# Rows of C copied by four DMAs each, and the first group's softplus summed in PSUM

## What is computed

```
delta = softplus(dt @ dt_proj.T + dt_proj_b)
A = -exp(A_log)
for each position t:
    dA = exp(delta_t[:, None] * A)
    h  = dA * h + (delta_t * u_t)[:, None] * B_t[None, :]
    y_t = sum over the states n of h[:, n] * C_t[n]
y = (y + u * D) * silu(z)
```

## Time and profile before

| | us |
|---|---|
| median of three runs | 427.69 |
| lowest and highest | 424.73, 428.63 |
| the profiled execution | 426.04 |
| its span in the profile | 424.3 |

### The profile page before, as it was taken

The page is one execution under the profiler, slowest core; times in us unless marked ns, Lnnn a source line. Parts: engine busy times, 40 slices in busy tenths (PEclk is TensorE's granted clock), DMA queues, the critical chain, the costliest instruction groups (busy, mean ns, idle before and its releaser), DMA issues.

```text
span 424.3 us, 11081 instructions
## 1 busy us (share of the span) xinstructions
PE 368.8 (87%) x4065; PEld 254.5 (60%) x4065; DVE 306.4 (72%) x631; ACT 286.9 (68%) x600; POOL 166.5 (39%) x142
## 2 busy tenths in 40 slices
PE   5799999999999597989499775998978989999996
PEld 4577777777755243444154342453954579888885
DVE  2869887698664989888269889985758957555554
ACT  3588899999967868759646793359974364444443
POOL 8314132232201438833985899970722400000000
PEclk9969999999999999999979999999999989999998
DMA  7120000002314272462222222200020001111111
GB/s 160 9 21 8 2 3 1 0 0 56 76 28 108 106 175 101 129 160 98 102 103 102 103 80 102 105 12 0 14 65 2 2 1 23 19 20 22 21 22 27
DMA packets 28496, 23.23 MB, mean 55 GB/s; under 512 B 20928, under 2 KB 22720, under 8 KB 28464
## 3 DMA queue, kind: packets, MB, share of 16 engines
q1 hardware_dynamic: 28068, 22.77, 19.8%
q10 hardware_dynamic: 396, 0.05, 0.1%
HBM read 2.00 MB, written 1.61 MB: 9 GB/s over the span
## 4 chain that ended last, share of the span: by engine, by line
PE 38%; DVE 24%; issue 16%; ACT 9%; POOL 8%; DMA 3%; SPq 1%; DVEq 1%; ACTq 1%; POOLq 0%
PE pair L1683 6%; DVE pair L1976 3%; PE pair L1174 3%; POOL hC L542 3%; PE pair L1185 3%; PE pair L1134 3%; DVE stats L1757 3%; PE pair L1299 2%; DVE Ts L1867 2%; PE pair L1193 2%; PE pair L1671 2%; DMA vec<-in_L_conv_b_qkv 2%; PE pair L1156 2%; PE pair L1352 2%; PE pair L1228 2%
## 5 line engine op out<-in xcount | busy, mean ns | idle before, releaser
L542 POOL TENSOR_TENSOR hC<-Hs,Cs 128x784 f32<-128x784 f32 x31 | 59.6, 1929 | 38.4 <-DVE Hs L1988 17.3
L510 POOL TENSOR_TENSOR Km<-Ks,mask 128x784 f32<-128x784 f32 x16 | 24.1, 1508 | 71.0 <-ACT Ks L717 71.0
L1352 PE MATMUL pair<-hC,ident 128*128 128x392 f32 x128 | 48.6, 504 | 1.3 <-POOL hC L542 1.2
L1861 DVE TENSOR_REDUCE mx<-pair 128x8 f32<-128x392 f32 x64 | 33.0, 556 | 19.3 <-PE pair L1134 19.2
L1976 DVE TENSOR_TENSOR pair<-DU,pair 128x392 f32<-128x392 f32 x64 | 35.6, 556 | 15.3 <-PE pair L1348 15.1
L1683 PE MATMUL pair<-hst,BD 128*128 128x112 f32 x224 | 37.7, 299 | 2.1 <-DVE Rt L2241 0.4
L1174 PE MATMUL pair<-ident,Pr 113*113 113x113 f32 x256 | 37.3, 280 | 2.5 <-issue 1.6
L1174 PEld LDWEIGHTS pair<-ident,Pr 113*113 113x113 f32 x256 | 31.2, 184 | 12.8 <-issue 12.0
L1348 PE MATMUL pair<-BCf,sel 96*128 96x392 bf16 x64 | 21.8, 343 | 16.6 <-DVE Hs L1988 9.7
L1988 DVE TENSOR_TENSOR_SCAN Hs<-dA,Hs,pair 128x392 f32<-128x392 f32 x32 | 33.0, 1030 | 3.6
L1683 PEld LDWEIGHTS pair<-hst,BD 128*128 128x128 f32 x224 | 30.0, 195 | 9.1 <-DVE hst L2235 5.2
(11 more groups left out here) (254 smaller groups left out, 840.8 us busy)
## 6 DMA issues: line engine op xcount, KB each, us to landing
Cs<-BCf SPq DMA_DIRECT2D x32, 392.0 KB
SX<-XP SPq DMA_DIRECT2D x16, 336.8 KB, 5.9
XT<-in_x SPq DMA_DIRECT2D x4, 392.0 KB, 7.0
out<-Os SPq DMA_DIRECT2D x28, 56.0 KB, 1.7
AD<-Aa SPq DMA_DIRECT2D x4, 196.0 KB
NB<-in_L_conv_x_proj_w SPq DMA_DIRECT2D x4, 3.0 KB
DW<-in_L_conv_dw SPq DMA_DIRECT2D x4, 1.1 KB
W<-in_L_conv_w_qkv ACTq DMA_DIRECT2D x1, 48.0 KB
```

What stands on the lines that cost most here:

```text
L542: eng.tensor_tensor(hC[:, i % NHC, :], Hs[:, i % NHS, :], Cs[i % NCS][:, :], ALU.mult).then_inc(v_c, 1)
L1352: return eng.matmul(STATES[:, h, :], ident[:, :], src[:, columns(h)], start=first, stop=last)
L1861: eng.tensor_reduce(mx[:, g, :], banks[g][:, 0:392].rearrange("p (m k) -> p m k", k=WT), AX.X, ALU.max).then_inc(max_r, 1)
```

## The change

Each row of C is copied by four DMAs, one for each image, instead of one. All waits for the copies count four times the increments. In the first group's softplus, max(x, 0) stays in PSUM where x lay. The remainder is made behind the attention's last residual instead of ahead of it; it is subtracted before the wait for the logarithm, and the logarithm is added last, which writes `DL`. The first `total` waits for that (`v_dl`), since it overwrites the PSUM pair.

```diff
@@ -437,7 +437,9 @@
                         eng.wait_ge(c_["xB"], c + 1)
                     if i >= NCS:
                         eng.wait_ge(v_c, i - NCS + 1)
-                    eng.dma_start(Cs[i % NCS][:, :], bcast(BCf[3 * C + n:P:DS, c % 2, :], 1, C)).then_inc(s_cs[i % NCS], 16)
+                    for g in range(G):
+                        row = 3 * C + DS * g + n
+                        eng.dma_start(Cs[i % NCS][C * g:C * g + C, :], bcast(BCf[row:row + 1, c % 2, :], 1, C)).then_inc(s_cs[i % NCS], 16)
 
             shifted_copies(0)
             shifted_copies(1)
@@ -535,7 +537,7 @@
 
                 for n in states:
                     i = DS * c + n
-                    eng.wait_ge(s_cs[i % NCS], 16 * (i // NCS + 1))
+                    eng.wait_ge(s_cs[i % NCS], 16 * G * (i // NCS + 1))
                     eng.wait_ge(v_s, 2 * i + 2)
                     if i >= NHC:
                         eng.wait_ge(y_s, i - NHC + 1)
@@ -617,7 +619,7 @@
                     scaled(2)
                     pads()
                     times_c(3, 5, 6)
-                    eng.wait_ge(s_cs[(DS * J - 1) % NCS], 16 * (DS * J // NCS))
+                    eng.wait_ge(s_cs[(DS * J - 1) % NCS], 16 * G * (DS * J // NCS))
                     eng.wait_ge(v_b, 2 * DS * J)
                     eng.wait_ge(v_c, DS * J - 1)
                     eng.memset(AD[:], 0.0).then_inc(t_zz, 1)
@@ -1359,7 +1361,7 @@
                     if n == 0 and c:
                         eng.wait_ge(v_y2, c)
                     elif n == 0:
-                        eng.wait_ge(a_m, 1)
+                        eng.wait_ge(v_dl, 1)
                     for h in range(2):
                         ins = add_up(hC[:, i % NHC, :], h, n == 0, n == DS - 1)
                     ins.then_inc(y_s, 1)
@@ -1955,17 +1957,18 @@
             def first_rows():
                 eng.wait_ge(p_["xB"], 1)
                 eng.tensor_copy(halves(BCf[:, 0, :]), result("xB", 0)).then_inc(c_["xB"], 1)
-                remainder(0)
 
             eng.wait_ge(c_["delta"], 2)
-            eng.tensor_scalar(halves(DL[:, 0, :]), result("delta", 0), vec[:, V_DTB:V_DTB + 1], 0.0, ALU.add, ALU.max).then_inc(a_m, 1)
+            first = result("delta", 0)
+            eng.tensor_scalar(first, first, vec[:, V_DTB:V_DTB + 1], 0.0, ALU.add, ALU.max).then_inc(a_m, 1)
             dve_att(17, 1, first_rows)
+            remainder(0)
             eng.wait_ge(a_m, 1)
+            eng.wait_ge(v_cc, 1)
+            eng.tensor_tensor(first, first, halves(rest), ALU.subtract).then_inc(g_ml, 1)
             eng.wait_ge(a_l, 1)
-            eng.tensor_tensor(DL[:, 0, :], DL[:, 0, :], sp[:, SP_L, :], ALU.add).then_inc(g_ml, 1)
             eng.wait_ge(g_ml, 1)
-            eng.wait_ge(v_cc, 1)
-            eng.tensor_tensor(DL[:, 0, :], DL[:, 0, :], rest, ALU.subtract).then_inc(v_dl, 1)
+            eng.tensor_tensor(halves(DL[:, 0, :]), first, halves(sp[:, SP_L, :]), ALU.add).then_inc(v_dl, 1)
             eng.wait_ge(v_dl, 1)
             eng.tensor_tensor(DU[:, 0, :], DL[:, 0, :], US[:, 0, :], ALU.mult).then_inc(v_du, 1)
 
@@ -2070,7 +2073,7 @@
 
 
             c, i = J - 1, DS * J - 1
-            eng.wait_ge(s_cs[i % NCS], 16 * (DS * J // NCS))
+            eng.wait_ge(s_cs[i % NCS], 16 * G * (DS * J // NCS))
             eng.wait_ge(v_s, 2 * DS * J)
             eng.wait_ge(y_s, i - NHC + 1)
             for h in range(2):
```

## The result

| | us |
|---|---|
| before, median of 4 runs | 427.61 (424.73 to 428.63) |
| after, median of 4 runs | 470.41 (468.69 to 472.07) |
| ratio after to before | 1.101, 95% interval 1.095 to 1.108 |
| the profiled execution after | 468.69, span 467.0 |

A forecast was written before the change was run, and what follows sets the result against it. Rows of C, copied by four engines, were taken to pace the state stage. Profiled 426.04 us plus 66 for slower rows, minus 0 for the softplus, gave 492, forecast as 493 us; range 426 to 600 us.

The forecast's parts named there:

- What bounds the stage: State stage: copies of rows of C, 3.94 us each, 32 taking 126 us, are one of two things setting its pace.
- 16 engines for a piece: Copies of C: each piece, with outermost dimension 32, spreads over 16 DMA engines where a row had 4.
- The outlet: Reads of C: one source partition lies behind one outlet giving 24.5 GB/s, however many engines ask; a piece takes 4.1 us.
- The cost of a row: State stage: a row of C takes 6.0 us instead of 3.94, adding 66 us over 32 rows.
- in step: Copies of C: all engines at one outlet at a time, 24.5 GB/s, so 16.4 us a row.
- 0.6 of the way: Copies of C: engines' assumed drift from one outlet at a time towards four side by side, giving 68.6 GB/s.
- SP's issues: SP's queue: four issues a row take 2.2 us instead of 0.55, below a row's 3.94, so not the next limit.
- The softplus: First group's softplus: DL is whole 1.1 us earlier, bounds 0.2 to 2.2; likeliest effect at the end 0.
- The sum: Whole kernel: profiled 426.04 + 66 - 0 = 492 us; forecast 493, as the median of runs is 1.65 more.
- B: Rival for the rows of C: engines stay in step, 9.5 to 16.4 us a row, some 830 us in full; chance 0.11.
- C: Rival for the rows of C: engines wholly apart over four outlets, 3.9 to 4.2 us a row, 424 to 436 us; chance 0.12.
- D: Rival: no shared limit for one partition, row in 2.0 us, VectorE's 7.95 us stall goes, 418.6 us; chance 0.10.

The follow-up runs named there:

- e3: The changed kernel, but each of the four DMAs of a row reads 32 different partitions of US instead of one row of C 32 times: 419.4 us.
- e8: The changed kernel, but each group's 32 rows of C are first written to DRAM and the four DMAs of a row read from there: 418.4 us.
- e5: The changed kernel, but all four pieces of every row read neighbouring partitions 96 to 99 instead of partitions 8 apart: 769.6 us.
- e9: The changed kernel, but each row's pieces read two source partitions, the other two being read in the next row: 584.8 us.
- e10: As e8, rows of C read from DRAM, but with one DMA for each row instead of four: 435.0 us.
- e6: The changed kernel, but rows are read in state order 0 4 1 5 2 6 3 7, so successive rows have other source partitions: 470.6 us.
- e7: The kernel before with the new softplus order, and three small DMAs issued behind each row's one DMA without waiting for them: 428.5 us.
- e2: The kernel before with only the new order of the first softplus, one DMA a row: 426.8 us, ratio 1.000.
- e1: The kernel before with only the four DMAs for each row of C and the old softplus: 469.4 us, ratio 1.099.

## Why the prediction was right, step by step

*What bounds the stage.* Right. The rows of C paced it: faster ones gave 7 and 9 us (e3, e8), slower ones about 32 times their excess (change, e5, e9).

*16 engines for a piece.* Right: the share of the DMA engines is 0.94 where it was 0.26.

*The outlet.* The mechanism is shown by e3 (no shared outlet) and e5 (nothing but one). Its rate was taken too low, 24.5 instead of 27.0 GB/s: 24.5 is what one engine had in the kernel before, and e10 has 24.3 an engine from DRAM, so it was taken from rows in which the engines and not the outlets may be what limits.

*The cost of a row.* This is the term that was mis-sized: 6.0 us was forecast, 5.2 to 5.3 measured. 32 x (5.31 - 3.94) = 44 us, where 66 was forecast and 42.8 came. Most of the miss is the outlet's rate. With 27.0 GB/s an outlet, in step is 27 GB/s and apart 108 (an estimate: no run shows four outlets giving four times one), and 0.6 of the way is 75.6 GB/s or 5.3 us a row; 77 was measured. But that 0.6 fits is luck, since its reason was wrong. Not 16 pieces are queued but about four (e9; e6 gains nothing), which happen to lie at four outlets. e9, with the same depth and two outlets at a time, gave 45 GB/s.

*SP's issues.* "2.2 us, below a row" was right as a price (e3: 592 ns; e7: no loss beyond 0.7%), but they took 1328 ns. I hadn't said that a full queue shows up as long issues, and in the chain they look like the cause.

*The softplus.* 1.1 us at the front was forecast, 1.0 measured, and nothing at the end (e2). e1 and the whole change differ by 1 us in the other direction, which is within their intervals.

*The sum.* 426.04 + 43.8 = 469.8 with the measured row; 468.69 was the profiled execution. (The forecast's own 492 + 1.65 is 493.7, put down as 493.) So close an agreement is partly chance. With the 5.2 us of the rate the sum is 467, and the traces have the stage 45 us longer (from the first issue of a row to VectorE's last product, 136.3 to 282.2 before and 133.7 to 324.9 after) and what stands ahead of it 2.6 us shorter, for no reason that they show. PE's clock was lower in the longer stage, 0.86 against 0.98. What that costs wasn't separated, but it isn't the main cause: in e5 and e9 the clock was lower still (0.60 and 0.73 in their windows), and the rows' excess alone gives 351 us where 342 were measured, and 159 where 159 were.

*The rivals.* B's full bound needs one outlet for all, and e5 shows what that costs. C would have needed pieces wholly apart; with four on their way they give 77 GB/s. D's condition, rows in 2 us, was about met in e3 and e8: 419.4 and 418.4 us, where D said 418.6. The stall of 7.95 us that D wanted gone was 1.54 in e8.

## What to carry to other kernels

When a share of the DMA engines stands at an odd fraction (0.26) and GB/s is flat, ask both how many engines the outermost dimension gives and how many outlets the source partitions lie behind; raising only the first made it worse. A broadcast of a few SBUF rows to all partitions is bound at its source, and a detour through DRAM that costs one more DMA a group removed it; but the write must not stand behind long transfers in the same queue (2.0 us to landing in e8, 13.1 in e10). Long issues on SP are a sign of transfers ahead that don't land, so change what they read before moving the issues.

## What was unexpected in the hardware

- Four neighbouring partitions gave 27.0 GB/s together to 16 engines (e5); partitions 8 apart gave 77 GB/s with four pieces on their way.
- SP had 4.0 to 4.3 pieces on their way in the change, e5 and e9, whatever their duration, and in the kernel before about four whole rows, four times as large; the issue is what grew longer (0.54 us at least, 4.98 at most in e5).
- 16 engines reading the same 3 KB in DRAM, 32 times a piece, didn't slow each other in a way seen here: a piece lands in 2.4 us, 2.2 us with 32 source partitions in SBUF.
- An issue of such a read from DRAM took 421 ns at the median, one from SBUF 592 (e8 and e3).
